# Causal masks added by the fused maximum on VectorE, and scores of 64-wide heads in pairs of row tiles

## The chip, the cores and the metric

The kernel runs on one core of one Trainium2 chip. The metric is device time in microseconds of one execution, from inputs in HBM to the output in HBM. TensorE, VectorE, ScalarE, GpSimd and SyncE each run their own stream of instructions; they meet only at semaphores.

## What is computed

Two layers of a "macaron" network over activations of 4 sequences x 512 tokens x 256 features. In order: attention with 64-wide heads and rotary positions (32 query heads, 8 key/value heads, causal over all 512 keys), a mixture of 16 experts, an attention with 8-wide heads and no mask; then the 64-wide attention and the experts once more, a gated block, an attention with 128-wide heads (16 query, 4 key/value heads, each block of 128 queries sees its own and the previous block of keys), and the gated block again. The part that matters here:

```
scores = einsum('bqhd,bkhd->bhqk', q, k) / sqrt(HEAD_DIM)
scores = where(causal, scores, -1e30)      # 128-wide: where(j >= p and j <= p + 128)
attn   = softmax(scores, -1)
o      = einsum('bhqk,bkhd->bqhd', attn, v)
```

Matrices are multiplied in split precision: each fp32 operand is kept as a rounded high part and a low part, and three products (high x high, low x high, high x low) replace one.

## The kernel before, in words

`Plan` writes one list of steps by hand. Every engine's program walks the whole list in that order and issues its share of each step, so the list fixes the order on each engine, and an engine that waits holds back everything behind it.

`Plan.attention` plans the attentions; `wide` is true for 128-wide heads. The 64-wide attention stands twice in the program ("narrow" here). It runs over 4 chunks `c` of heads x 4 sequences `b`: 16 units. A unit of the narrow attention has 8 groups, `(t, g)`: 4 query tiles `t` of 128 tokens, 2 key/value heads `g`. A group has 4 query heads `j`. It reads `o.w = (t + 1) * 128` keys. A unit of the wide attention has 4 groups of 4 heads with 128 or 256 keys. Inside a group, `Plan.attention` interleaves: the scores of this group's heads one at a time; `normalise` and `turn` (division by the sum, then the transposes of the probabilities, one step per 128 keys `kt`) of the group before; `weigh` (probabilities x values, column tiles of 64, every second group) and `project_out`; and four times `beside`, which issues pieces of the next unit's preparation (`q_product`, `q_rotate`, `k_rotate`, `v_copy` in one group; `q_turn`, `k_turn`, `k_low` and an empty piece in another). In the narrow attention TensorE has work in the first two of these four pieces only.

One head goes like this. TensorE writes scores into one PSUM bank (`scores`, L1442 on). Narrow: the transposed query tile holds the high part in partitions 0 to 63 and the low part in 64 to 127, one slot per head (copies L1712, L1713 on ScalarE, L1882, L1883 on VectorE); keys are stored twice, in both halves. So two products over 128 rows do the work of three: L1457 (times the high part of the keys) and L1458 (times the low part). A third product, L1461, adds the mask: a bfloat16 identity times 128 (wide: 256) columns of -1e30 and 0. VectorE takes the negated row maximum (L1895), ScalarE the exponential with its sum (L1723), which also frees the bank. `exponentials()` puts the exponentials of all waiting heads into the list at the place where it is called.

The banks for scores are a ring, `sring`: 3 for the narrow attention, 2 for the wide one. Head n of the narrow attention may start when the exponential of head n - 3 has ended. `tring` (2 banks) serves the transposes, which L1728 copies out; `wring` (3) serves the rest.

## Time and profile before

| | |
|---|---|
| median of 3 runs | 4043.11 us (4032.47 to 4050.41) |
| profiled execution, its time | 4029.73 us |
| span of the profiled execution | 4028.0 us |
| TensorE matmul busy | 3451.3 us, 86% |
| VectorE busy | 2704.4 us, 67% |
| ScalarE busy | 2025.5 us, 50% |
| granted TensorE clock, mean | 0.91 of full |
| narrow attentions | from about 50 to 1000 us and 1925 to 2870 us |
| wide attention | from about 3340 to 3910 us |

Busy time is the sum of the recorded durations of an engine's instructions. Matmuls overlap: a row's duration holds the time through the array, so the price of a matmul in a stream is the distance from its start to the next start. In the timelines, a bracket gives the idle time of the engine before the instruction and who ended it.

### The profile page before, as it was taken

To read this page: it belongs to the slowest core of one execution; us is meant where nothing else is said; L and a number is where in the kernel's file an instruction comes from. 1 tells how busy PE (TensorE), PEld (TensorE's weight loads), DVE (VectorE), ACT (ScalarE), POOL (GpSimd) and SP (SyncE) were. 2 spreads that over 40 slices of the span, in tenths; PEclk is the share of its full clock that TensorE was granted. 3 is DMA by queue.
4 is the path that set the end of the run, shared out by engine and by line. 5 is a ranking of instruction groups with operands and counts; after the bars stand their busy time and mean duration, and the time that the engine had idled before them with its cause. 6 is when DMAs were issued, how large, how long until landed. Compare 5 with 4: busy or idle time off the path is not lost. (4 is left out here: it accounts for less than half of the span.)

```text
span 4028.0 us, 61413 instructions
## 1 busy us (share of the span) xinstructions
PE 3451.3 (86%) x21258; PEld 2352.0 (58%) x21258; DVE 2704.4 (67%) x7549; ACT 2025.5 (50%) x5389; POOL 993.7 (25%) x964
## 2 busy tenths in 40 slices
PE   6899999887798599897789999988699668999986
PEld 4677677665454233343567767766455346788864
DVE  6788888775343677783778888876444456677766
ACT  4667767654222165665566767665322113455441
POOL 3211112232354100012121212123244332222213
PEclk9999999988899588998999999998799768999997
DMA  3140400011754322202050300001375500000010
GB/s 118 64 138 1 158 1 1 18 43 50 189 90 79 98 53 53 58 10 83 3 200 2 129 29 1 1 32 44 105 153 89 133 13 1 14 14 4 1 31 21
DMA packets 203899, 234.54 MB, mean 58 GB/s; under 512 B 20358, under 2 KB 190280, under 8 KB 202824
## 3 DMA queue, kind: packets, MB, share of 16 engines
q1 hardware_dynamic: 172648, 190.48, 15.5%
q0 software_dynamic: 30944, 40.14, 5.9%
q8 instruction: 172, 2.82, 0.3%
q14 instruction: 135, 1.11, 0.1%
HBM read 96.03 MB, written 133.73 MB: 57 GB/s over the span
## 5 line engine op out<-in xcount | busy, mean ns | idle before, releaser
L1723 ACT ACTIVATE p_prob<-bank,p_small 128x256 f32<-128x256 f32 (+3 forms) x1280 | 654.2, 517 | 240.0 <-DVE p_small L1895 223.6
L1895 DVE TENSOR_REDUCE p_small<-bank 128x1 f32<-128x256 f32 (+3 forms) x1280 | 586.8, 465 | 240.3 <-PE bank L1461 231.2
L1728 ACT ACTIVATE p_prT<-bank 128x512 f32<-128x512 f32 x752 | 420.3, 601 | 365.3 <-PE bank L1469 360.5
L2241 POOL TENSOR_TENSOR p_tm<-p_rope_a,p_rope_b 128x512 f32<-128x512 f32 x192 | 245.4, 1278 | 1437.6 <-DVE p_rope_b L1872 1420.7
L1469 PE MATMUL bank<-g_ident,p_prob 128*128 128x128 f32 x3008 | 440.8, 286 | 42.0 <-DVE p_prob L1904 21.4
L1457 PE MATMUL bank<-p_k,p_q 128*128 128x256 f32 (+2 forms) x1024 | 423.4, 414 | 53.8 <-ACT p_prob L1723 53.8
L1904 DVE TENSOR_SCALAR p_prob<-p_prob,p_small 128x256 f32<-128x256 f32 (+3 forms) x1280 | 417.1, 389 | 11.3
L1478 PE MATMUL bank<-p_prT,p_v 128*64 128x512 f32 (+1 forms) x1504 | 412.8, 604 | 0.2 <-ACT p_prT L1728 0.2
L1941 DVE TENSOR_REDUCE p_nmax<-bank 128x1 f32<-128x512 f32 x512 | 325.0, 684 | 101.1 <-PE bank L1519 95.6
L1469 PEld LDWEIGHTS bank<-g_ident,p_prob 128*128 128x128 f32 x3008 | 352.3, 147 | 63.6 <-DVE p_prob L1904 27.1
L1751 ACT ACTIVATE p_prT<-bank 128x512 f32<-128x512 f32 x512 | 278.0, 596 | 154.7 <-PE bank L1531 154.5
L1458 PE MATMUL bank<-p_k,p_q 128*128 128x256 f32 (+2 forms) x1024 | 339.8, 332 | 0.0
L1427 PE MATMUL bank<-p_w_hi,p_aT_hi 128*128 128x512 f32 (+1 forms) x768 | 298.8, 389 | 47.3 <-DVE p_aT_lo L1836 30.8
L1652 PE MATMUL bank<-p_w,p_hT 128*128 (+1 forms) x632 | 331.2, 607 | 0.2
L1461 PE MATMUL bank<-p_mask,g_identb 128*128 128x128 bf16 (+1 forms) x1280 | 310.1, 242 | 0.0
L1429 PE MATMUL bank<-p_w_lo,p_aT_hi 128*128 128x512 f32 (+1 forms) x768 | 267.0, 348 | 0.0
L1428 PE MATMUL bank<-p_w_hi,p_aT_lo 128*128 128x512 f32 (+1 forms) x768 | 267.0, 348 | 0.0
L1723 ACT ACTIVATION_READ_ACCUMULATOR p_prob<-bank,p_small 128x1 f32 x1280 | 265.8, 208 | 0.0
L1457 PEld LDWEIGHTS bank<-p_k,p_q 128*128 128x128 f32 x1024 | 203.4, 199 | 85.1 <-ACT p_prob L1723 71.1
L1490 PE MATMUL bank<-p_o_hi,p_oT_hi 128*128 128x256 f32 x768 | 233.9, 305 | 5.8 <-DVE p_oT_lo L1909 5.8
L1427 PEld LDWEIGHTS bank<-p_w_hi,p_aT_hi 128*128 128x128 f32 x768 | 151.9, 198 | 140.8 <-issue 76.3
L1869 DVE TENSOR_TENSOR p_rope_a<-bank,p_cos 128x512 f32<-128x512 f32 (+1 forms) x384 | 185.2, 482 | 69.1 <-PE bank L1429 69.0
(304 smaller groups left out, 7234.2 us busy)
## 6 DMA issues: line engine op xcount, KB each, us to landing
sorted<-p_blank SPq DMA_DIRECT2D x32, 2304.0 KB, 18.9
p_w<-in_L_ffn_w SPq DMA_DIRECT2D x96, 256.0 KB, 4.6
p_h_in<-sorted SPq DMA_DIRECT2D x158, 144.0 KB, 2.7
p_k_st<-k_saved SPq DMA_DIRECT2D x16, 288.0 KB
p_q_st<-q_saved SPq DMA_DIRECT2D x16, 288.0 KB
g_stage<-in_L_ffn_wq SPq DMA_DIRECT2D x8, 512.0 KB, 4.3
g_stage<-in_L_ffn_wo SPq DMA_DIRECT2D x16, 256.0 KB, 4.9
second_sum<-g_res SPq DMA_DIRECT2D x8, 512.0 KB, 5.6
```

Source lines behind the costliest of these rows:

```text
L1427: pe.matmul(use.ap[:, 0:n], hi, whi[:, k, cols(c0, n)], start=k == 0, stop=False)
L1457: pe.matmul(bank[:, 0:n], q[:, head, :], khi, start=True, stop=False)
L1458: pe.matmul(bank[:, 0:n], q[:, head, :], klo, start=False, stop=False)
L1461: pe.matmul(bank[:, o.w - mw:o.w], identb[:, :], A.mask[:, 2 * P - mw:2 * P], start=False, stop=True).then_inc(s.use.full[0].sem)
L1469: ins = pe.transpose(s.use.ap[:, j * P:(j + 1) * P], o.probs[j].ap[:, s.kt * P:(s.kt + 1) * P], ident[:, :])
L1478: ins = pe.matmul(s.use.ap[cols(o.g * A.hd, A.hd), :], o.u.v.ap[:, o.k0 + kt, cols(o.g * A.hd, A.hd)], o.prT[kt].ap, start=kt == 0, stop=k ...
L1652: ins = pe.matmul(o.up.ap, o.hT.ap[:, k * P:(k + 1) * P], w_all(A)[:, bass.ds(at + k * 2 * H, 2 * H)], start=k == 0, stop=k == KC - 1)
L1723: act.activation(s.prob.ap[:, 0:s.o.w], s.use.ap[:, 0:s.o.w], ACT.Exp, bias=sm[:, 0, j:j + 1], accum_out=sm[:, 1, j:j + 1]).then_inc(s.use ...
L1728: act.activation(s.prT.ap, s.use.ap, ACT.Copy).then_inc(s.use.free[0].sem)
L1895: dve.tensor_reduce(s.o.sm.ap[:, 0, s.j:s.j + 1], s.use.ap[:, 0:s.o.w], axis=AX.X, op=ALU.max, negate=True).then_inc(made)
L1904: dve.tensor_scalar(o.probs[j].ap[:, 0:o.w], o.probs[j].ap[:, 0:o.w], o.sm.ap[:, 2, j:j + 1], None, ALU.mult).then_inc(made)
L1941: dve.tensor_reduce(A.nmax[:, s.qt % 2, s.t, s.r, s.g % 2:s.g % 2 + 1], s.use.ap, axis=AX.X, op=ALU.max, negate=True).then_inc(s.use.free[ ...
```

## The change

Three edits, in all three attentions of these two kinds.

1. The mask product (L1461) and its bfloat16 identity go. VectorE's maximum becomes a `tensor_tensor_reduce`: it adds the mask (bfloat16, in SBUF; for narrow heads now 512 columns wide) to the scores, multiplies by -1, writes the result back over the scores in PSUM, and folds the minimum, which is the negated maximum. The exponential takes `scale=-1.0`.
2. Narrow: the query tile is laid out as the wide one: slots 0 to 3 high part, 4 to 7 low part, two heads per slot, one in partitions 0 to 63, the other in 64 to 127. One copy on ScalarE and one subtraction on VectorE over 128 partitions replace two each over 64.
3. Narrow: `scores` takes two heads at a time, (0, 1) and then (2, 3). TensorE waits for both banks, then issues three rounds, each with one product of 64 rows for either head: row tiles 0 to 63 and 64 to 127, different banks. The call for (0, 1) stands where head 0 stood and the call for (2, 3) where head 2 stood, ahead of `turn` for the key tiles 2 and 3; their exponentials come where those of head 2 came, behind these turns. Wide heads keep their order and their three products.

```diff
+        def scores(o, *heads):
             s = self.step("scores", A)
-            s.o, s.j, s.use, s.prob = o, j, sring.take(), prob.take()
+            for j in heads:
+                h.o, h.j, h.use, h.prob, h.max_made = o, j, sring.take(), prob.take(), self.vector_made.up()
+                waiting.append(h)
...
-                scores(cur, 0)
+                scores(cur, *((0,) if wide else (0, 1)))
...
-                scores(cur, 1)
+                if wide:
+                    scores(cur, 1)
...
                 exponentials()
-                scores(cur, 2)
+                scores(cur, *((2,) if wide else (2, 3)))
                 beside()
...
                 for kt in range(2, nturn):
                     turn(prev, kt)
                 exponentials()
-                scores(cur, 3)
-                exponentials()
+                if wide:
+                    scores(cur, 3)
+                    exponentials()
                 beside()
```

```diff
 # TensorE
-            w.wait_ge(s.use.before, *s.ready)
...
-                pe.matmul(bank[:, 0:n], q[:, head, :], khi, start=True, stop=False)
-                pe.matmul(bank[:, 0:n], q[:, head, :], klo, start=False, stop=False)
-            mw = min(o.w, 2 * P) if A.wide else P
-            w.wait_ge(A.masked)
-            pe.matmul(bank[:, o.w - mw:o.w], identb[:, :], A.mask[:, 2 * P - mw:2 * P],
-                      start=False, stop=True).then_inc(s.use.full[0].sem)
+            w.wait_ge(*(h.use.before for h in s.heads), *s.ready)
+            for i, (qp, kp) in enumerate(((0, 0), (4, 0), (0, 1))):
+                for h in s.heads:
+                    rows = slice(0, P) if A.wide else cols(h.j % 2 * A.hd, A.hd)
+                    at = qp + (h.j if A.wide else (o.g * KV + h.j) // 2)
+                    ins = pe.matmul(h.use.ap[:, 0:n], q[rows, at, :], k[rows, kp, o.g, keys], start=i == 0, stop=i == 2)
+                    if i == 2:
+                        ins.then_inc(h.use.full[0].sem)
 # VectorE
-            dve.tensor_reduce(s.o.sm.ap[:, 0, s.j:s.j + 1], s.use.ap[:, 0:s.o.w], axis=AX.X, op=ALU.max,
-                              negate=True).then_inc(made)
+            for h in s.heads:
+                x = h.use.ap[:, 0:o.w]
+                w.wait_ge(h.use.full, o.sm.after)
+                dve.tensor_tensor_reduce(x, x, A.mask[:, A.mask.shape[1] - o.w:], -1.0, FAR, ALU.add, ALU.min,
+                                         o.sm.ap[:, 0, h.j:h.j + 1]).then_inc(made)
```

## Rows read from the trace of the kernel before

**Rows 1.** Windows: length, busy us of PE, PEld, DVE, ACT, POOL, clock, DMA share, GB/s
```profile
300.00:400.00 100.00, 95.01 (x636) 71.54 (x635) 84.58 (x220) 72.62 (x199) 15.77 (x15) 1.00 0.00 1
...
3600.00:3700.00 100.00, 98.85 (x650) 81.26 (x650) 72.42 (x226) 50.04 (x162) 20.88 (x24) 1.00 0.00 1
```

**Rows 2.** Timeline, TensorE: first matmul of a narrow unit and of the next
```profile
341.61 0.37 PE L1457 MATMUL bank<-p_k,p_q 128*128 128x256 f32 x1
...
394.92 0.36 PE L1457 MATMUL bank<-p_k,p_q 128*128 128x256 f32 x1
```

**Rows 3.** Timeline, TensorE: a narrow head over 512 keys, and the next
```profile
439.07 0.48 PE L1457 MATMUL bank<-p_k,p_q 128*128 128x512 f32 x1
439.38 0.40 PE L1458 MATMUL bank<-p_k,p_q 128*128 128x512 f32 x1
439.62 0.23 PE L1461 MATMUL bank<-p_mask,g_identb 128*128 128x128 bf16 x1
439.74 0.50 PE L1457 MATMUL bank<-p_k,p_q 128*128 128x512 f32 x1
```

**Rows 4.** Timeline, all engines: 256-column heads, then a wait for a bank
```profile
355.48 0.36 PE L1457 MATMUL bank<-p_k,p_q 128*128 128x256 f32 x1
...
355.84 0.36 PE L1457 MATMUL bank<-p_k,p_q 128*128 128x256 f32 x1
...
356.26 0.36 ACT L1723 ACTIVATE p_prob<-bank,p_small 128x128 f32<-128x128 f32 x1
...
356.76 0.38 PE L1457 MATMUL bank<-p_k,p_q 128*128 128x256 f32 x1 [0.36 <-ACT p_prob L1723]
```

**Rows 5.** Timeline, TensorE: into the column tiles of `weigh` and out
```profile
348.81 0.23 PE L1461 MATMUL bank<-p_mask,g_identb 128*128 128x128 bf16 x1
348.97 3.65 PE L1478 MATMUL bank<-p_prT,p_v 128*64 128x512 f32 x16
352.56 0.50 PE L1427 MATMUL bank<-p_w_hi,p_aT_hi 128*128 128x512 f32 x1
```

**Rows 6.** Timeline, TensorE: row tiles in the attention with 8-wide heads
```profile
1501.47 0.50 PE L1531 MATMUL bank<-p_q_st,p_k_st 26*128 26x512 f32 x1
1501.47 0.50 PE L1519 MATMUL bank<-p_k_st,p_q_st 24*128 24x512 f32 x1
...
1501.91 0.39 PE L1541 MATMUL bank<-p_zero 128*128 128x256 bf16 x2
```

**Rows 7.** Timeline, weight loads: the load for L1458, beside the first row of Rows 3
```profile
439.15 0.19 PEld L1458 LDWEIGHTS bank<-p_k,p_q 128*128 128x128 f32 x1
```

**Rows 8.** Timeline, TensorE: a mask product of a wide head, and what follows
```profile
3592.49 0.28 PE L1461 MATMUL bank<-p_mask,g_identb 128*128 128x256 bf16 x1
3592.61 0.59 PE L1478 MATMUL bank<-p_prT,p_v 128*128 128x512 f32 x1
```

**Rows 9.** Groups: line, shapes, count, busy us, mean ns, idle before
```profile
L1895 DVE TENSOR_REDUCE p_small<-bank 128x1 f32<-128x256 f32 x448 | 184.7, 417 | 43.1 <-PE bank L1461 40.5
L1895 DVE TENSOR_REDUCE p_small<-bank 128x1 f32<-128x512 f32 x256 | 174.2, 687 | 92.8 <-PE bank L1461 91.1
L1723 ACT ACTIVATE p_prob<-bank,p_small 128x256 f32<-128x256 f32 x448 | 212.3, 476 | 161.9 <-DVE p_small L1895 155.5
L1723 ACT ACTIVATE p_prob<-bank,p_small 128x512 f32<-128x512 f32 x256 | 177.2, 700 | 10.6 <-DVE p_small L1895 5.0
L1883 DVE TENSOR_TENSOR p_q<-bank,p_q 64x512 fp32r<-64x512 f32 x128 | 88.9, 694 | 1.8
```

**Rows 10.** Timeline, VectorE: the fused operation in the experts
```profile
1097.67 0.17 DVE L2159 CUSTOM_DVE_ANT_0 p_pick<-p_h_in,p_one 128x16 f32<-128x16 f32 x1
1097.76 0.08 DVE L2159 DVE_READ_ACCUMULATOR2_ANT p_gate<- 128x1 f32 x1
```

**Rows 11.** Timeline, TensorE and ScalarE: two key tiles transposed, then copied
```profile
365.43 1.03 PE L1469 MATMUL bank<-g_ident,p_prob 128*128 128x128 f32 x8
...
366.07 1.09 ACT L1728 ACTIVATE p_prT<-bank 128x512 f32<-128x512 f32 x2 [1.90 <-PE bank L1469]
```

More of the change, by code:

```diff
@@ L167, in __init__ @@
         self.ident = top("ident", [P, P])
-        self.identb = top("identb", [P, P], BF16)
         self.half = top("minus_half", [P, NT])
@@ L204, in constants @@
         s = self.step("constants")
-        s.zeroed = [self.pool_made.up() for _ in range(2)]
-        s.made = [self.pool_made.up() for _ in range(3)]
+        s.zeroed = self.pool_made.up()
+        s.made = [self.pool_made.up() for _ in range(2)]
         self.constants_made = s.made[-1]
@@ L314, in attention @@
         A.lnw = sb("lnw", [P, KC])
-        A.mask = sb("mask", [P, 2 * P], BF16)
+        A.mask = sb("mask", [P, 2 * P if wide else S], BF16)
         if not wide:
@@ L323, in attention @@
         A.const = s.count.up(32 if wide else 48)
-        s.zeroed, s.right, A.masked = (self.pool_made.up() for _ in range(3))
+        s.zeroed, A.masked = self.pool_made.up(), self.pool_made.up()
+        if wide:
+            A.masked = self.pool_made.up()
         w_ready, o_ready, w_used, o_used = {}, {}, {}, {}
@@ L451, in group @@
             return o
-        def scores(o, j):
+        def scores(o, *heads):
             s = self.step("scores", A)
-            s.o, s.j, s.use, s.prob = o, j, sring.take(), prob.take()
-            s.ready = [o.u.q_made[o.t], o.u.k_made[max(1, o.t)]]
-            s.max_made = self.vector_made.up()
-            o.probs.append(s.prob)
-            o.scored = s.use.full
-            waiting.append(s)
+            s.o, s.heads, s.ready = o, [], [o.u.q_made[o.t], o.u.k_made[max(1, o.t)]]
+            for j in heads:
+                h = Phase()
+                h.o, h.j, h.use, h.prob, h.max_made = o, j, sring.take(), prob.take(), self.vector_made.up()
+                s.heads.append(h)
+                o.probs.append(h.prob)
+                o.scored = h.use.full
+                waiting.append(h)
         waiting = []
@@ L590, in attention @@
                 exponentials()
[L591 to L592 removed]
+                if wide:
+                    scores(cur, 3)
+                    exponentials()
                 beside()
@@ L1444, in tensor_program @@
         elif s.kind == "scores":
-            o, j, bank = s.o, s.j, s.use.ap
+            o = s.o
             n = max(o.w, 2 * P)
@@ L1893, in vector_program @@
         elif s.kind == "scores":
-            w.wait_ge(s.use.full, s.o.sm.after)
-            dve.tensor_reduce(s.o.sm.ap[:, 0, s.j:s.j + 1], s.use.ap[:, 0:s.o.w], axis=AX.X, op=ALU.max,
-                              negate=True).then_inc(made)
+            o = s.o
+            w.wait_ge(A.masked)
+            for h in s.heads:
[3 more added lines that the diff above has]
+                                         o.sm.ap[:, 0, h.j:h.j + 1]).then_inc(made)
         elif s.kind == "normalise":
@@ L2225, in pool_program @@
             w.wait_ge(own.turn())
-            pool.affine_select(out=A.mask[:, P:], in_=A.mask[:, P:], compare_op=ALU.is_ge, fill=NEG, base=0,
+            last = A.mask[:, A.mask.shape[1] - P:]
+            pool.affine_select(out=last, in_=last, compare_op=ALU.is_ge, fill=NEG, base=0,
                                pattern=[[-1, P]], channel_multiplier=1).then_inc(made)
-            w.wait_ge(own.turn())
-            pool.affine_select(out=A.mask[:, :P], in_=A.mask[:, :P], compare_op=ALU.is_ge, fill=NEG, base=0,
-                               pattern=[[1, P]], channel_multiplier=-1).then_inc(made)
+            if A.wide:
+                w.wait_ge(own.turn())
+                pool.affine_select(out=A.mask[:, :P], in_=A.mask[:, :P], compare_op=ALU.is_ge, fill=NEG, base=0,
+                                   pattern=[[1, P]], channel_multiplier=-1).then_inc(made)
         elif s.kind == "normed":
```

37 lines of the change are left out of this document (8 added, 29 removed).

## The prediction

> **What bounds the kernel now.** I read the table by slices first: the granted clock and the busy shares differ from stage to stage, so an edit is worth what it is worth in its own stage. Then the windows inside the stages that the change touches. In the steady part of the narrow attention TensorE is busy 95.0 of 100 us at full clock, VectorE 84.6, ScalarE 72.6; in the wide one TensorE is busy 98.9 [rows 1]. Both stages are bound by TensorE's order of work: what it does, plus what it waits for. Next the distance between the first matmuls of successive units: a narrow unit takes 394.92 - 341.61 = 53.3 us [rows 2], and there are 32 such units (2 attentions, 16 each). 5.0% of that, 2.7 us, is TensorE idle. Last the timeline around such a pause: a head that wants a bank waits until the exponential that holds it has ended [rows 4]. That wait is what the change rearranges.
>
> Prices on TensorE come from starts. A 512-column product takes 0.24 us of the stream, the mask behind it 0.12, a whole head 0.67 at its longest, as the first product behind a mask loses time to its weights (0.31 to the next start) [rows 3]; I take 0.64. A 256-column head takes 0.36 [rows 4], hence 0.12 for a product. For 384 columns I take the middle, 0.49 a head and 0.18 a product.
>
> **TensorE's work in a narrow unit.** Before: 16 heads x 0.36 (tiles 0 and 1 both stream 256 columns) + 8 x 0.49 + 8 x 0.64 = 14.8 us. After: 16 pairs of 3 rounds, 8 x 0.36 + 4 x 0.54 + 4 x 0.72 = 8.0 us, if the two row tiles run at once. Row tiles do so in the attention with 8-wide heads: two start in the same hundredth of a microsecond and take 0.50 each, as a lone one would [rows 6].
>
> But this visit to another tiling has a price. There a round of one 512-column product per tile holds the array from 1501.47 to 1501.91, 0.44 us, against 0.24 in a stream: 0.20 for weights that were not loaded ahead and for the array running empty at the end [rows 6]. Around `weigh` the same shows from outside: it starts 0.16 after the mask product, where the gap is otherwise 0.04 to 0.12, and the product behind it takes 0.50 instead of 0.40 [rows 3, 5]. So 0.2 us for each change of tiling. A unit has 16 visits, 32 changes. 4 fall away because the pair (0, 1) stands right before `weigh`, which changes tiling anyway. 8 fall away in the four groups where the group before had at most 2 key tiles: there nothing of TensorE stands between the pair (2, 3) and the next (0, 1). 20 x 0.2 = 4.0 us. TensorE's work shrinks by 14.8 - 8.0 - 4.0 = 2.8 us a unit. More than half of the gain in products and masks is eaten by changes of tiling.
>
> **The waits for banks.** With three banks and heads in pairs, the next group's pair (0, 1) needs the banks of this group's heads 1 and 2. Head 2 is scored last, together with head 3, and its exponential stands last too. Before, head 0 of the next group needed head 1 only, two heads back. So after the pair (2, 3) TensorE must wait for maximum and exponential of head 2, and what could cover it, the last two pieces of `beside`, holds no TensorE work in the narrow attention. Behind the wait are queued the pair itself, `weigh`, the products of the next unit and all transposes.
>
> The chain without cover: through the array 0.16 (0.40 of duration less 0.24 [rows 3]), 0.04 to VectorE, the maximum, 0.02 for the end of its accumulator read, 0.04 to ScalarE (three estimates, bounded by 0 and by the 0.14 that comes next), the exponential, and 0.14 until TensorE goes on (from 356.26 + 0.36 to 356.76 [rows 4]). The maximum of 256 keys takes 0.417, of 512 keys 0.687, the exponentials 0.476 and 0.700 [rows 9]; 128 keys: 0.28 by the same slope and 0.36 [rows 4]; 384: 0.55 and 0.59, the middles. Four groups have no cover: 128 keys 1.04, 256 keys twice 1.29, 384 keys 1.54; 5.2 us. In the other four, the turns of key tiles 2 and 3 stand between, but their copies stand ahead of the exponential on ScalarE. The first copy starts 0.64 after the first transpose, two copies take 1.09 and the next instruction starts about 0.1 before their end [rows 11]; 8 transposes cost TensorE 0.88 (1.03 less the 0.15 through the array), 4 cost 0.44. Two tiles: 0.64 + 0.97 + exponential 0.70 + 0.14 - 0.88 = 1.57, and with 128 keys 1.23. One tile: 0.64 + 0.5 + 0.14 - 0.44 + exponential = 1.43 (384 keys) and 1.54 (512). Sum 5.8.
>
> In addition the divisions of the group before stand behind two maxima instead of one on VectorE, 0.76 us later with 512 keys. In `q_turn` groups little TensorE work lies ahead of the transposes that need them: I add 0.9 us a unit for tiles 2 and 3, bounds 0 and 1.5. Waits after: 5.2 + 5.8 + 0.9 = 11.9 us against 2.7.
>
> **VectorE and ScalarE.** The fused operation is in the trace on 16 elements: 0.17 us, and the accumulator read starts 0.09 behind it and ends with it [rows 10]. So it adds little latency, but some 0.07 of VectorE a head: 32 x 0.07 = 2.2 us a unit. The low part of the queries saves one of two subtractions of 0.694 us, four times a unit, 4 x 0.63 = 2.5 us in a stream [rows 9]; ScalarE saves four copies of about 0.55, the size of those in [rows 11]. VectorE stays at 0.846 x 53.3 = 45 us a unit: even. No row shows the fused operation reading PSUM, taking a bfloat16 mask and writing PSUM. From below its rate is that of the plain maximum; no mechanism makes it faster. From above I take twice the time an element. I choose the lower end, since the only row of the operation has the fixed cost of a plain one.
>
> The smaller edits (bfloat16 identity, one select less, a mask of 512 columns) lie before the first scores, on GpSimd, and are costed at nothing, at most 1 us.
>
> **Wide.** 256 mask products go, 0.12 each [rows 8], 31 us, on an engine that is 98.9% busy [rows 1]. The order of heads stays. Shorter work on TensorE can make the waits on its two banks show: 15 to 31 us remain; I take 31.
>
> **Sum.** A regular narrow unit: 11.9 - 2.7 - 2.8 = +6.4 us. 24 units (chunks 0 to 2) give 154. In the 8 units of the last chunk the steps of the router hold TensorE between the same steps already, and a bank wait beside such a hold costs nothing; I take 4 of 6.4: 32. Narrow +186, wide -31: +155 us. On the profiled execution, 4029.7 us (span 4028.0), that is 4185; its time lies 13 under the median of the runs, so against the median 4043 + 155, rounded 4200. The sum is good to about a third of its waits: 11.9 could be 9 (-90 us over 32 units) or 14 (+67).
>
> **A rule of the skill on weights.** In the stream before, the weights for L1458 load at 439.15, while L1457 has run since 439.07 over the same 128 rows [rows 3, 7]: loads are hidden behind matmuls of the same rows, and I cost the rounds inside a visit so. The Trainium skill (TensorE: Matmul & The Clock Gate, "The mechanism" under packing small matmuls) says that a weight load overlaps running matmuls only when the row group differs. No row shows two rounds on the same row tile. If loads there were not hidden, as a mechanism of this kernel, each pair would pay its second and third load openly, 0.1 each (the 0.50 against 0.40 of [rows 3, 5]): 512 pairs x 0.2 = +102 us, 4300. That page's rule leads there; the trace contradicts it for full rows.
>
> **The rivals.**
> *Faster (0.10).* The waits in front of (0, 1) stay what they are, 2.7 us a unit, because maximum and exponential of head 2 are through by the time TensorE is: then 32 x 2.8 + 31 = 121 us are gained, 3920. For it: TensorE is the bound, and the masks are pure work on it. Against: the chain of two engines cannot be shorter than its two rows, and nothing covers it. It decides at waits of 2.7 + 2.8 + 1.0 (the wide gain per unit) = 6.5 us a unit, 0.8 per group; my smallest is 1.04.
> *No change (0.05).* The waits come to about that 6.5: 4025 to 4060.
> *The fused operation at half rate (0.07).* Write-back to PSUM adds 0.27 us for 256 keys, 0.53 for 512: about 1.8 us a unit in the open chains and, with 11 us more on VectorE, its own 56 us a unit come close to the period. About +4 us a unit, 4330.
> *Weights in the open (0.07).* 4300, as above.
> *Clock (0.07).* It is 1.00 in these windows [rows 1]; with pauses of 1.5 us in every group it could fall for parts of them. A tenth of 1700 us at half speed is +85 or so: 4285.
> *The pairs don't run together (0.02).* Then 8.0 us of rounds become 16: +256, 4455.
> *The forecast (0.62).* 4110 to 4290, likeliest 4200.
>
> **Numbers.** 0.5%, about what a measurement of this kernel can tell from no change, is 20 us. Slower: 0.62 + 0.07 x 3 + 0.02 = 0.85; same 0.05; faster 0.10. The range 4110 to 4320 holds forecast, clock and weights, and part of the half-rate case: about 0.8.
>
> **What would show it.** In the timeline of a narrow unit: a period near 60 us; TensorE idle before the first product of most groups until ScalarE's exponential, 1 to 1.6 us; that wait at the top of the list of waits, some 250 to 350 us in all. The two products of a round start together, rounds 0.12 or 0.24 apart, next work 0.1 to 0.2 late. The fused operation within 0.1 of the old maximum, a read of about 0.08. VectorE's busy time about even, ScalarE's lower by some 70 us (128 copies of 0.55). A wide unit shorter by up to 16 x 0.12 = 1.9 us. I am wrong if the pause after the pair (2, 3) is under 0.8 us, if rounds run slower than 0.24, or if the wide stage does not shrink.

## The result, and the profile after

| | before | after |
|---|---|---|
| median, same chip | 4046.76 us | 4240.01 us (4230.17 to 4249.77) |
| profiled execution | 4029.73 us | 4230.17 us |
| span | 4028.0 us | 4228.4 us |
| granted clock, mean | 0.913 | 0.909 |
| TensorE busy | 3451.3 us | 3395.0 us |
| VectorE busy | 2704.4 us | 2640.1 us |
| ScalarE busy | 2025.5 us | 1942.9 us |

The changed kernel takes 1.0482 of the time before (95% interval 1.0441 to 1.0523): 4.8% slower, where +155 us, 3.8%, was forecast. All three engines do less and the kernel takes longer, so the loss is waiting.

Measured from the first to the last score product of a stage in the two profiled executions: the two narrow attentions take 934.7 -> 1052.4 and 933.2 -> 1043.7 us (+228 together), the wide one 550.8 -> 530.9 (-20), everything else 1609.3 -> 1601.4 (-8). That is the 200 us between the spans.

The windows, in steady parts of a narrow and of the wide attention (columns as in [rows 1], which answers to them):

```profile
700.00:800.00 100.00, 82.12 (x566) 57.73 (x568) 71.16 (x249) 58.89 (x172) 14.06 (x14) 1.00 0.00 1
```
```profile
3800.00:3900.00 100.00, 98.19 (x633) 81.71 (x632) 75.39 (x279) 52.00 (x168) 20.98 (x24) 1.00 0.00 1
```

TensorE was busy 95.0 of 100 us in the narrow stage and is 82.1 now, at full clock. In the wide one it was 98.9 and is 98.2. What TensorE waits for stands on top of its list of waits (who waits, for whom, us in total, times, longest); before, this wait came to 53.8 us in 124 times:

```profile
PE bank L1460 <- ACT p_prob L1717: 318.7, 285, 2.8
PE bank L1625 <- DVE p_n_tiles L2061: 45.0, 18, 3.0
```

L1460 is the score product now, L1717 the exponential. A narrow unit, from its first matmul to that of the next, takes 807.01 - 747.45 = 59.6 us, against 53.3 in [rows 2]; a wide unit 3874.74 - 3842.01 = 32.7, against 34.05 before. Timeline, TensorE:

```profile
747.45 0.62 PE L1460 MATMUL bank<-p_k,p_q 64*128 64x256 f32 x6 [1.36 <-ACT p_prob L1717]
```
```profile
807.01 0.77 PE L1460 MATMUL bank<-p_k,p_q 64*128 64x256 f32 x6 [1.35 <-ACT p_prob L1717]
```
```profile
3842.01 0.99 PE L1460 MATMUL bank<-p_k,p_q 128*128 128x256 f32 x6
```
```profile
3874.74 0.76 PE L1460 MATMUL bank<-p_k,p_q 128*128 128x256 f32 x4
```

One open chain with 384 keys, all engines. The pair (2, 3) of a group is scored at 719.70, and the next group's pair (0, 1) follows at 721.91:

```profile
719.70 0.80 PE L1460 MATMUL bank<-p_k,p_q 64*128 64x384 f32 x6
720.53 0.57 DVE L1887 CUSTOM_DVE_ANT_0 bank<-bank,p_mask 128x384 f32<-128x384 f32 x1 [0.65 <-PE bank L1460]
721.01 0.14 DVE L1887 DVE_READ_ACCUMULATOR2_ANT p_small<- 128x1 f32 x1
721.01 0.60 DVE L1887 CUSTOM_DVE_ANT_0 bank<-bank,p_mask 128x384 f32<-128x384 f32 x1
721.19 0.58 ACT L1717 ACTIVATE p_prob<-bank,p_small 128x384 f32<-128x384 f32 x1 [0.73 <-DVE p_small L1887]
...
721.91 0.79 PE L1460 MATMUL bank<-p_k,p_q 64*128 64x384 f32 x6 [1.42 <-ACT p_prob L1717]
```

TensorE's row of six products ends at 720.50, VectorE begins 0.03 later, ScalarE follows 0.18 after the read's start, and TensorE goes on 0.14 after the exponential's end: 1.42 us in which TensorE has nothing that it may issue. The bank is head 2's; head 3's maximum runs beside it and holds nobody up.

The two engines whose work was exchanged, grouped by line and shape (columns as in [rows 9]):

```profile
L1887 DVE CUSTOM_DVE_ANT_0 bank<-bank,p_mask 128x256 f32<-128x256 f32 x448 | 185.6, 438 | 88.7 <-PE bank L1460 87.0
L1887 DVE DVE_READ_ACCUMULATOR2_ANT p_small<- 128x1 f32 x1280 | 181.7, 142 | 0.0
...
L1887 DVE CUSTOM_DVE_ANT_0 bank<-bank,p_mask 128x512 f32<-128x512 f32 x256 | 172.6, 716 | 169.5 <-PE bank L1460 169.5
```
```profile
L1896 DVE TENSOR_SCALAR p_prob<-p_prob,p_small 128x512 f32<-128x512 f32 x256 | 137.3, 600 | 2.3
```

The fused operation takes 438 and 716 ns where the plain maximum took 417 and 687 [rows 9], although it reads a mask and writes 128 x 512 scores back to PSUM. The division of 512 elements (L1896), which was not touched, went from 483 to 600 ns in the mean. Nothing in the forecast allowed for that; the trace leads to it below.

### The profile page after: what moved, and what is told of

The parts are those of the page before. It is cut to its first block and busy times, and to the rows that moved or that the text cites. A ratio compares the mean times of both kernels' runs of the same rounds, so it can differ in the third digit from the quotient of the medians.

```text
span 4228.4 us, 62424 instructions
## 1 busy us (share of the span) xinstructions
PE 3395.0 (80%) x21000; PEld 2237.8 (53%) x21002; DVE 2640.1 (62%) x8701; ACT 1942.9 (46%) x5261; POOL 992.5 (23%) x960
## 5 line engine op out<-in xcount | busy, mean ns | idle before, releaser
L1887 DVE CUSTOM_DVE_ANT_0 bank<-bank,p_mask 128x256 f32<-128x256 f32 (+3 forms) x1280 | 585.4, 491 | 509.9 <-PE bank L1460 482.6
L1460 PE MATMUL bank<-p_k,p_q 64*128 64x256 f32 (+3 forms) x3840 | 537.2, 354 | 325.6 <-ACT p_prob L1717 318.7
L1717 ACT ACTIVATE p_prob<-bank,p_small 128x256 f32<-128x256 f32 (+3 forms) x1280 | 644.7, 511 | 248.3 <-DVE p_small L1887 238.7
L1460 PEld LDWEIGHTS bank<-p_k,p_q 64*128 64x128 f32 (+1 forms) x3840 | 346.0, 193 | 449.1 <-ACT p_prob L1717 392.5
L1469 PE MATMUL bank<-g_ident,p_prob 128*128 128x128 f32 x3008 | 476.2, 292 | 48.5 <-DVE p_prob L1896 29.6
L1896 DVE TENSOR_SCALAR p_prob<-p_prob,p_small 128x256 f32<-128x256 f32 (+3 forms) x1280 | 426.5, 397 | 11.3
L1478 PE MATMUL bank<-p_prT,p_v 128*64 128x512 f32 (+1 forms) x1504 | 423.0, 620 | 0.2 <-ACT p_prT L1722 0.2
L1726 ACT ACTIVATE p_oT_hi<-bank 128x512 fp32r<-128x512 f32 x192 | 114.8, 598 | 391.6 <-PE bank L1478 370.8
L1717 ACT ACTIVATION_READ_ACCUMULATOR p_prob<-bank,p_small 128x1 f32 x1280 | 260.9, 204 | 0.0
L1491 PE MATMUL bank<-p_o_hi,p_oT_lo 128*128 128x256 f32 x768 | 225.5, 294 | 0.0
```

Of the source, the lines that this page charges most:

```text
L1460: ins = pe.matmul(h.use.ap[:, 0:n], q[rows, at, :], k[rows, kp, o.g, keys], start=i == 0, stop=i == 2)
L1469: ins = pe.transpose(s.use.ap[:, j * P:(j + 1) * P], o.probs[j].ap[:, s.kt * P:(s.kt + 1) * P], ident[:, :])
L1478: ins = pe.matmul(s.use.ap[cols(o.g * A.hd, A.hd), :], o.u.v.ap[:, o.k0 + kt, cols(o.g * A.hd, A.hd)], o.prT[kt].ap, start=kt == 0, stop=k ...
L1717: act.activation(s.prob.ap[:, 0:s.o.w], s.use.ap[:, 0:s.o.w], ACT.Exp, bias=sm[:, 0, j:j + 1], scale=-1.0, accum_out=sm[:, 1, j:j + 1]).th ...
L1887: dve.tensor_tensor_reduce(x, x, A.mask[:, A.mask.shape[1] - o.w:], -1.0, FAR, ALU.add, ALU.min, o.sm.ap[:, 0, h.j:h.j + 1]).then_inc(made)
L1896: dve.tensor_scalar(o.probs[j].ap[:, 0:o.w], o.probs[j].ap[:, 0:o.w], o.sm.ap[:, 2, j:j + 1], None, ALU.mult).then_inc(made)
```

## The experiments

Ratios are to the kernel before on the same chip, with the 95% interval. fused_only, fused_paired, after_4banks and covered ran on one chip in one batch; row_single, after_one_bank_less, after_exp_first and fused_exp_first on another; the last three ran on the first chip in a later batch. Where two runs of different batches are compared, both intervals count. "Unit" is the distance between the first matmuls of two successive narrow units in the steady part, 53.3 before and mostly 59.5, some 61.0, after. The theory: the loss comes from the order in pairs, in which head 2's bank is needed at once and nothing covers its chain. Against it stood the fused operation (rate, read, PSUM write), the row tiles (weights in the open, visits) and, once the traces were compared, VectorE's divisions.

**fused_only.** The fused maximum alone; heads one by one, products over 128 rows and the old query layout as before.

```diff
-                scores(cur, *((0,) if wide else (0, 1)))
+                scores(cur, 0)
...
+            for h in s.heads:
+                parts = ((h.j, 0), (4 + h.j, 0), (h.j, 1)) if A.wide else ((o.g * KV + h.j, 0), (o.g * KV + h.j, 1))
+                for i, (at, kp) in enumerate(parts):
+                    ins = pe.matmul(h.use.ap[:, 0:n], q[:, at, :], k[:, kp, o.g, keys], start=i == 0, stop=i == len(parts) - 1)
...
```

> The fused maximum alone: the order, the layout of the queries and the two products over 128 rows are those of the kernel before, heads one by one; only the mask products are gone and VectorE adds the masks. My theory (the order of the pairs costs the time, the fused maximum gains): TensorE loses 32 x 0.12 us of mask products a narrow unit and up to 1.9 us a wide unit, VectorE gains 2 us of work a unit; narrow unit 50 to 51.5 us instead of 53.3, wide unit 32.7 instead of 34.05, the whole 3920 to 3975 us. Rival (the fused operation, with its accumulator read, puts VectorE on the path in the narrow attention): narrow unit 53 to 56 us, the whole 4020 to 4110.

3951.97 us, ratio 0.9838 (0.9813 to 0.9862), unit 51.65. This is faster than both kernels. The gain of 1.65 us a unit is less than the masks' 32 x 0.12 = 3.8: TensorE is busy 2.7 us less in a steady unit (50.82 -> 48.11) and idle 1.0 us more (2.49 -> 3.52). A mask product in front of other work was worth less than 0.12: a lone head of 512 keys holds TensorE for 0.62 us before and 0.55 now, one of 256 keys 0.29 and 0.24 (medians of 94 and 154). And shorter heads wait longer for their banks (53.8 us in 124 times -> 86.1 in 140):

```profile
PE bank L1457 <- ACT p_prob L1719: 86.1, 140, 0.7
```

The rate of the fused operation and the mask from SBUF are cleared: the kernel that has them alone gains.

**fused_paired.** The same and the order in pairs, no row tiles and no new layout.

```diff
-                scores(cur, 0)
+                scores(cur, *((0,) if wide else (0, 1)))
...
-                scores(cur, 1)
+                if wide:
+                    scores(cur, 1)
...
-                scores(cur, 2)
+                scores(cur, *((2,) if wide else (2, 3)))
...
-                scores(cur, 3)
-                exponentials()
+                if wide:
+                    scores(cur, 3)
+                    exponentials()
```

> As the changed kernel, in its order of pairs, with the fused maximum, but the queries and the products over 128 rows of the kernel before: two products a head, no row tiles, no change of tiling. Theory (the bank wait behind the pair (2, 3) is the loss, not the row tiles): scores cost 10.6 us a narrow unit instead of 12.0, the waits stay; narrow unit 57.5 to 59.5 us, the whole 4170 to 4240. Rival (the row tiles and their changes of tiling are the loss): narrow unit near 51, the whole near 3960.

4237.26 us, ratio 1.0555 (1.0523 to 1.0587), unit mostly 62.0, some 60.4 and some 63.6, which is more than the 57.5 to 59.5 expected. Its wait is that of the changed kernel:

```profile
PE bank L1459 <- ACT p_prob L1721: 346.7, 289, 1.9
```

The order alone takes 0.9838 to 1.0555, 7.2 points or 285 us on one chip. Row tiles and the merged copies then bring back some 0.7 points: 1.0555 against 1.0482, two intervals that touch. The traces show where: a pair of 512 keys holds TensorE for 1.03 us in fused_paired and for 0.89 in the changed kernel, one of 384 keys 0.78 and 0.72, one of 256 keys 0.58 and 0.55.

**row_single.** The reverse: row tiles, new layout, but heads one by one.

```diff
-                scores(cur, *((0,) if wide else (0, 1)))
+                scores(cur, 0)
...
-                if wide:
-                    scores(cur, 1)
+                scores(cur, 1)
...
-                if wide:
-                    scores(cur, 3)
-                    exponentials()
+                scores(cur, 3)
+                exponentials()
```

> The changed kernel with heads one by one in the order of before: same layout of the queries, same 64-row products, three a head, but never two heads at once. Theory: no bank wait of the new kind, but 16 x 0.36 + 8 x 0.54 + 8 x 0.72 = 15.8 us of products and up to 32 visits to the row tiling at 0.4 us, 11 us net of neighbours, against 14.8 us of scores before: narrow unit 61 to 64 us, ratio 1.06 to 1.09. Rival (a visit to the row tiling costs TensorE next to nothing, and only the bank wait made the loss): narrow unit 51 to 53 us, ratio 0.98 to 1.00.

4166.34 us, ratio 1.0308 (1.0272 to 1.0344), unit 57.4: between the theory's range and the rival's. TensorE is busy 96 of 100 us and waits little, but with products that a single head cannot overlap:

```profile
300.00:400.00 100.00, 96.05 (x590) 65.48 (x590) 72.34 (x253) 61.21 (x176) 14.02 (x14) 1.00 0.00 1
```
```profile
701.38 0.96 PE L1458 MATMUL bank<-p_k,p_q 64*128 64x512 f32 x3
702.27 0.66 PE L1467 MATMUL bank<-g_ident,p_prob 128*128 128x128 f32 x4
702.86 0.97 PE L1458 MATMUL bank<-p_k,p_q 64*128 64x512 f32 x6
703.76 0.65 PE L1476 MATMUL bank<-p_prT,p_v 128*64 128x512 f32 x2
```

A lone head of 512 keys holds TensorE for 0.89 us, of which three products are 0.72; two heads issued one behind the other hold it for 0.90, so heads on different row tiles overlap even when they are issued in turn. A visit costs 0.17 beyond its rounds; its first product starts 0.20 after a transpose and 0.33 after a product of 512 columns, where it is 0.03 and 0.23 in fused_only. That is 0.27 to 0.35 a visit, less than the 0.4 (entry and exit) that the expectation of 61 to 64 used, and the expectation had no heads of two calls overlapping. Against fused_only (unit 51.6) the scores, with their third product, hold TensorE for 2.9 us a unit more, the work around them for 4.1 more, and it waits 1.3 less.

**after_4banks.** The changed kernel with four score banks in place of three, one fewer for the rest.

```diff
-        n_s = 2 if wide else 3
+        n_s = 2 if wide else 4
```

> The changed kernel with 4 banks for narrow scores instead of 3, and 2 instead of 3 for the other results. Theory: the pair (0, 1) needs only heads 0 and 1 of the group before, whose exponentials are long through; the 319 us of TensorE waiting for exponentials fall under 60, a narrow unit takes 49 to 54 us (the upper part is for what the missing third bank costs), the whole 3920 to 4070. Rival (the row tiles, or the fused operation's latency, make the time): within 1% of 4240.

4193.18 us, ratio 1.0437 (1.0418 to 1.0457), unit 58.9 to 60.4. The wait on exponentials fell from 318.7 to 7.4 us, as the theory says, but the unit fell far short of the 49 to 54 us expected. By the ratio the gain is 0.4 points, which lies within the 1% that the rival gave; so this run alone does not tell the two apart. Other waits stand in place of the one that fell:

```profile
PE bank L1447 <- DVE p_q L1872: 102.1, 88, 1.2
PE bank L1433 <- DVE p_rope_b L1866: 57.7, 35, 2.2
PE bank L1490 <- ACT p_v L1703: 47.1, 84, 0.7
PE bank L1433 <- DVE p_oT_lo L1901: 41.6, 56, 0.9
```

All four are waits for the banks of the remaining two. The run mixed two things, so the next one took them apart.

**after_one_bank_less.** Three score banks and two for the rest.

```diff
-        sring, tring, wring = (Banks(self.banks[i:j]) for i, j in ((0, n_s), (n_s, n_s + 2), (n_s + 2, 8)))
+        sring, tring, wring = (Banks(self.banks[i:j]) for i, j in ((0, n_s), (n_s, n_s + 2), (n_s + 2, 8 if wide else 7)))
```

> Control for the run with 4 score banks: the changed kernel with 3 score banks and 2 banks for the other narrow results; the eighth bank is left unused in the narrow attentions. With 4 + 2 banks the waits of scores for exponentials vanished, but waits of 286 us for the two remaining banks stood in their place. Theory (both waits are real, and the score wait is worth its price where nothing else binds): this one has both kinds; narrow unit 63 to 66 us, the whole 4330 to 4450 at the level of this chip's before of about 4020. Rival (the score wait is no loss of its own, TensorE would be held by VectorE's and ScalarE's work anyway): narrow unit within 1 us of the 58.9 of the run with 4 + 2 banks, the whole within 1% of 4193.

4499.94 us, ratio 1.1156 (1.1134 to 1.1178), unit 67 to 69.5, more than the 63 to 66 expected. At two other banks the fourth score bank is worth 1.1156 - 1.0437 = 7.2 points; at three score banks the third other bank is worth 1.1156 - 1.0482 = 6.7. A score bank more is worth about the whole cost of the order, and so is a bank for the rest: the kernel has no bank to give. That a ninth bank would take the loss away is argued from these differences, not shown; and whether a fourth score bank would also help heads issued one by one was not run.

**after_exp_first.** Head 2's and 3's exponentials ahead of the turns of key tiles 2 and 3.

```diff
+                if not wide:
+                    exponentials()
                 for kt in range(2, nturn):
                     turn(prev, kt)
                 exponentials()
```

> The changed kernel with one call moved: in narrow groups the exponentials of heads 2 and 3 stand ahead of the turns of key tiles 2 and 3 instead of behind them, so ScalarE does them ahead of the copies. Theory by the sum of the forecast: the four groups without such turns stay as they are; in the other four the copies leave the chain, 0.97 us in two groups, 0.5 us in two, less what the copies themselves then come late: narrow unit 57 to 58.5 instead of 59.5, ratio to before 1.030 to 1.042. If the order on ScalarE doesn't matter: 1.048.

4095.53 us, ratio 1.0154 (1.0123 to 1.0185), unit 56.4: more than the 1.030 to 1.042 that the expectation gave. TensorE's wait fell by 99 us:

```profile
PE bank L1462 <- ACT p_prob L1719: 219.8, 224, 1.5
```

3.3 of the 4.8 points hang on where ScalarE's copies of the turned probabilities stand. In the steady unit the four open waits are what they were (0.94, 1.18, 1.18, 1.42 us), and the four behind turns fell from 5.05 us to 1.91. That is 24 x 3.1 = 74 us from 59.5 to 56.4, of some 133. The last chunks of the two attentions give 39 us. The rest is in what changed beside it: no unit of 61 us is left, and the time at half clock in the narrow stages is 91 and 81 us in place of 137 and 126.

**covered.** The pair (2, 3) ahead of the second piece of `beside` and of all turns, its exponentials ahead of the copies.

```diff
+                if not wide:
+                    scores(cur, 2, 3)
                 beside()
+                if not wide:
+                    exponentials()
                 for kt in range(0, min(2, nturn)):
                     turn(prev, kt)
                 exponentials()
-                scores(cur, *((2,) if wide else (2, 3)))
+                if wide:
+                    scores(cur, 2)
```

> The changed kernel with another order in narrow groups: the pair (2, 3) right behind project_out, ahead of the second piece of preparation and of all turns, its exponentials ahead of the copies of the turns. So that piece (0.2 or 0.7 us) and all turns (0.4 to 1.8 us) stand between the pair (2, 3) and the next pair (0, 1). Theory: the wait for the exponential of head 2 is covered in most groups; a narrow unit takes 49.5 to 52.5 us, the whole 3910 to 4010. If the wait isn't the cause: within 1% of 4240.

4071.93 us, ratio 1.0138 (1.0109 to 1.0167), unit 57.0 to 59.0; 49.5 to 52.5 was expected. The cover works, and TensorE meets the next resource, the two banks of the transposes:

```profile
PE bank L1474 <- ACT p_prT L1727: 129.5, 119, 2.2
PE bank L1465 <- ACT p_prob L1722: 88.1, 113, 2.9
```

The copies that free the transposes' banks now stand behind two exponentials.

**covered_full.** The same order, products over 128 rows and the old query layout.

```diff
-            for i, (qp, kp) in enumerate(((0, 0), (4, 0), (0, 1))):
-                for h in s.heads:
-                    rows = slice(0, P) if A.wide else cols(h.j % 2 * A.hd, A.hd)
+            for h in s.heads:
+                parts = ((h.j, 0), (4 + h.j, 0), (h.j, 1)) if A.wide else ((o.g * KV + h.j, 0), (o.g * KV + h.j, 1))
...
```

> The order with the pair of heads 2 and 3 put ahead of the second projection piece and the turns (as in the run covered, ratio 1.0138), with products over 128 rows and no row tiles. The theory that the order sets the loss and that the row tiles and merged copies are worth 1 to 2.4 us of a narrow unit once the order is pairwise: unit 58 to 59.5 against 57.0, ratio 1.020 to 1.032. Rival: with its exponentials covered this order is bound by the tiling changes' visits, so without row tiles it gains: unit 55 to 56.5, ratio 0.998 to 1.012.

4116.38 us, ratio 1.0201 (1.0161 to 1.0240), unit 57.2 to 58.5 with some to 62. So row tiles and merged copies are worth some 0.6 points in this order too, as in the first pair of runs (0.7); the two intervals touch in both pairs, so the size is rough. The ratio lies at the low end of what the theory gave, and outside the rival's; the steady unit is shorter than the 58 to 59.5 of the theory. In the profiled executions the gain stands here in the last chunk (33 of 38 us), while in the first pair it stands in the other units (21 us) and the last chunk loses 29. Last chunks differ by some 12 us an attention between executions where their steps are the same (fused_split_moved below), so this split decides little.

**fused_exp_first.** The fused maximum alone, with the exponential of head 1 ahead of the first turns.

```diff
+                if not wide:
+                    exponentials()
                 for kt in range(0, min(2, nturn)):
                     turn(prev, kt)
                 exponentials()
```

> The fused maximum alone, heads one by one over 128 rows, with the exponential of head 1 ahead of the turns of key tiles 0 and 1 instead of behind them. The fused-only kernel waits 86 us on TensorE for exponentials, in 140 places, where head 0 of the next group needs the bank of head 1. Theory: that wait goes at the groups with one key tile, 30 to 80 us less: ratio to before 0.965 to 0.977 against 0.984. If TensorE is held by something else there (the copies of the turns, now late): 0.98 to 0.99.

3992.82 us, ratio 0.9896 (0.9879 to 0.9912), unit 52.3: worse than without (0.9838, 0.9813 to 0.9862), and not the 0.965 to 0.977 that the theory gave. The wait on exponentials halved (86.1 -> 40.1) and a new one took its place:

```profile
PE bank L1467 <- ACT p_prT L1726: 72.4, 87, 2.8
PE bank L1459 <- ACT p_prob L1721: 40.1, 90, 1.7
```

**after_split_moved and fused_split_moved.** For the units of 66 to 71 us that the forecast did not have: GpSimd's splits of the next block's weights (L2202) behind the first group of the unit with b = 2, in the changed kernel and in fused_only.

```diff
-            if b == 2 and c + 1 < NU:
-                split_qkv(c + 1, slot_qkv)
-                split_o(c + 1, slot_o)
...
                 prev = cur
+                if (t, g) == steps[0] and b == 2 and c + 1 < NU:
+                    split_qkv(c + 1, slot_qkv)
+                    split_o(c + 1, slot_o)
```

What led there is VectorE's timeline in such a unit of the changed kernel, and GpSimd's beside it, and TensorE's:

```profile
433.79 7.00 DVE L1896 TENSOR_SCALAR p_prob<-p_prob,p_small 128x512 f32<-128x512 f32 x4
```
```profile
434.54 3.48 POOL L2202 TENSOR_TENSOR p_w_lo<-g_stage,p_w_hi 128x1536 fp32r<-128x1536 f32 x1 [18.66 <-ACT p_w_hi L1690]
438.17 2.34 POOL L2202 TENSOR_TENSOR p_o_lo<-g_stage,p_o_hi 128x1024 fp32r<-128x1024 f32 x1
```
```profile
438.36 0.33 PE L1469 MATMUL bank<-g_ident,p_prob 128*128 128x128 f32 x1 [1.34 <-DVE p_prob L1896]
440.85 0.77 PE L1469 MATMUL bank<-g_ident,p_prob 128*128 128x128 f32 x5 [2.15 <-DVE p_prob L1896]
```

Four divisions of 512 elements take 7.00 us, while elsewhere in this kernel four take 1.67. The held ones end 0.3 us behind the two splits, and TensorE's transposes wait for them.

> The changed kernel with GpSimd's splits of the next attention block's weights placed behind the first group of the unit with b = 2 instead of ahead of that unit; nothing else differs. Theory: in the changed kernel the divisions of a group meet these splits on VectorE's and GpSimd's common memory path (four divisions in 7.00 us where others take 0.5 each), and this is what makes the units with b = 2 of the narrow attentions 66 to 71 us against 59.5 to 61. Moved, the splits meet matmul-bound or waiting stretches, the units fall to 60 to 62, and with six or so of them 30 to 45 us go: ratio to the kernel before 1.037 to 1.041. Rival: the splits only collide with other VectorE work in the later groups (copies out of banks, subtractions), so the loss moves along: ratio 1.045 to 1.052, and the unit stays at 66 to 71.

4206.89 us, ratio 1.0425 (1.0397 to 1.0452), against 1.0482 (1.0441 to 1.0523) unmoved. The two units at 432 and 680 us that took 66.1 and 67.3 take 61.0 and 59.5, the one of 71.1 takes 64.9. The spans differ by 27 us: the narrow attentions take 43 us less (2096.1 -> 2053.0), the wide one 2 less, and what lies outside the three attentions, where the edit changes nothing, 18 more. So the units bear the mechanism out. The ratio is just above the 1.037 to 1.041 expected, and its interval overlaps the unmoved one's. The collision itself did not go, it moved to divisions of 128 elements, and TensorE's waits for divisions fell from 29.6 to 20.0 us:

```profile
434.04 4.14 DVE L1896 TENSOR_SCALAR p_prob<-p_prob,p_small 128x128 f32<-128x128 f32 x4
```
```profile
434.62 3.47 POOL L2202 TENSOR_TENSOR p_w_lo<-g_stage,p_w_hi 128x1536 fp32r<-128x1536 f32 x1 [2.09 <-ACT p_w_hi L1690]
```

Four such divisions take 0.88 us when no split runs.

> The kernel with the fused maximum alone (heads one by one, products over 128 rows) and the same move of GpSimd's splits. Theory of the collision: long divisions (over 1 us) cost the kernel before some 13 us beyond their usual 0.48 us each, so at most about 10 us are to be had: ratio 0.981 to 0.984. Rival: heads one by one keep banks waiting for TensorE and not the other way round, the collision is covered, and the move gives nothing (0.984) or brings the splits into a stretch that was tight (up to 0.990).

3987.93 us, ratio 0.9878 (0.9858 to 0.9898): the rival. The units with b = 2 in the middle of fused_only already took 51.65, so nothing was there to be had, and after the move they take 52.6. The rest of what it lost, some 3 us a unit in the mean of the last chunks (267.5 -> 278.0 and 266.8 -> 280.9), where the step list is the same, I can't attribute. The kernel with heads one by one and the fused maximum alone, 0.9838, remains the best that was run.

## Why the forecast was right, and where its terms were off

**The waits (11.9 us a unit forecast).** The mechanism is what the traces show, and after_exp_first, fused_paired and the two bank runs each confirm a part of it. The unit was forecast at 59.7 and takes 59.5. The eight waits in front of a pair (0, 1) are 1.09, 0.94, 1.18, 1.18, 1.42, 1.25, 1.36 and 1.36 us in the unit at 747.45, 9.8 in all, against 10.9 in the forecast's sum; that sum counts 0.16 through the array in each, which the profile counts as busy, so on one count they agree within 0.2. The 0.9 us for late divisions is not what the trace shows: the other two waits of the unit come to 0.79 us, and a wait for the copies of turned probabilities (0.47 of it) was there before with 0.74. Windows of one steady unit, before and after:

```profile
341.61:394.92 53.31, 50.82 (x339) 37.59 (x338) 43.77 (x116) 37.07 (x106) 8.03 (x8) 1.00 0.00 1
```
```profile
747.45:807.01 59.56, 49.00 (x337) 34.07 (x337) 41.30 (x152) 34.47 (x101) 8.03 (x8) 1.00 0.00 1
```

TensorE's idle time rose by 8.1 us, where 9.2 were forecast, and its busy time fell by 1.8, where 2.8 were forecast. With the 8 x 0.16 = 1.3 us through the array counted as busy, the forecast says 7.9 and 1.5: two of its terms hold, not only their sum. That the unit comes out within 0.2 us is still partly luck, since the 0.9 for divisions stood for other waits.

**TensorE's work (-2.8 a unit forecast).** Right in kind. The pairs run together (the first two products of a pair start 0.003 us apart); of the rounds of 512 columns the second starts 0.33 behind the first, the third 0.23 behind the second. A pair over 512 keys, with the transposes of the next step behind it:

```profile
734.93 0.96 PE L1460 MATMUL bank<-p_k,p_q 64*128 64x512 f32 x6
735.82 0.44 PE L1469 MATMUL bank<-g_ident,p_prob 128*128 128x128 f32 x2
```

735.82 - 734.93 = 0.89, of which 0.72 are rounds. The other 0.17 lie half between the first two rounds and half behind the third. The entry costs 0.1 to 0.2 more (0.10 after a product of 512 columns, 0.18 after a transpose, by row_single against fused_only). So a visit costs 0.27 to 0.35, less than the 0.4 forecast, while masks in front of other work were worth less than the 0.12 taken (fused_only): two misses of opposite sign. The two experiments in pairs without row tiles put row tiles and merged copies at 0.6 to 0.7 points, 25 to 30 us. The forecast held visits to eat more than half of what row tiles save. In row_single visits, the third product, which a lone head can't overlap, and more time at half clock (331 us in the narrow stages against 193 in fused_only) together cost 4.7 points (1.0308 against 0.9838).

**The rule on weights.** The loads of a pair, and those for `weigh` behind it:

```profile
721.91 0.47 PEld L1460 LDWEIGHTS bank<-p_k,p_q 64*128 64x128 f32 x6 [1.74 <-ACT p_prob L1717]
722.63 0.20 PEld L1478 LDWEIGHTS bank<-p_prT,p_v 128*64 128x64 f32 x4 [0.25 <-issue]
```

The products of this pair start in rounds at 721.91, 722.19 and 722.37 and end at 722.70. All six loads are through at 722.38. The first round's products are in the array until 722.35, so those for the second and third round began while products over the same two row tiles were still in it. One distance is 0.10 longer than a round of 384 columns (0.28 against 0.17), not two, and that is in the 0.17 to 0.19 of a visit already. So the Trainium skill's rule (TensorE: Matmul & The Clock Gate, "The mechanism") that a load overlaps running matmuls only on another row group is not what this trace shows, for row tiles as for full rows, and the rival at 4300 us falls.

**VectorE.** The fused operation within 0.03 of the old maximum: right. The accumulator read was put at 0.08, from 16 elements [rows 10], and takes 0.142, always. It overlaps the next fused operation (both start at 721.01). In a steady unit of fused_only VectorE is busy 44.89 us against 43.77 before, so the fused operations cost 1.1 us a unit instead of the 2.2 forecast. In the changed kernel's unit it is 41.30, and VectorE's busy time, forecast about even, fell by 64 us in all. ScalarE fell by 83, forecast 70.

**The last chunk (4 us a unit forecast, 6.5 measured).** The 24 units of chunks 0 to 2 lost 176 us (154 forecast), the 8 of the last chunk 52 (32 forecast). In the second unit of that chunk the last six groups take 57.7 us before and 56.9 after. That seems to bear out the step "a bank wait beside such a hold costs nothing". But the granted clock there is 0.82 before and 0.92 after, 10.4 and 4.6 us of work lost, so the waits may have cost what the clock gave, and the step is not shown. The first two groups take 16.4 and then 22.3. Windows over these two groups, of before and of after:

```profile
778.30:783.30 5.00, 5.00 (x28) 4.39 (x28) 4.09 (x19) 1.78 (x6) 2.35 (x2) 0.73 0.09 30
783.30:794.70 11.40, 11.03 (x74) 7.62 (x72) 6.98 (x25) 5.26 (x18) 8.36 (x10) 1.00 0.26 92
```
```profile
877.00:899.30 22.30, 18.53 (x96) 12.57 (x96) 9.62 (x40) 7.01 (x24) 10.06 (x10) 0.80 0.15 53
```

By the granted clock, 0.20 of 22.3 us is 4.5 us of work lost to half clock, against 0.27 of 5.0 = 1.4 before: 3.1 of the 5.9. The others are pauses, 3.8 us idle against 0.4. So the forecast's 4 us left the clock out in a stretch where TensorE had just been held.

**What the forecast did not have.** The 176 us are 24 x 6.2 = 149 and 27 more. Part is the collision of divisions and splits: with the splits moved, chunks 0 to 2 take 33 us less. It was there before: the sum of what divisions of probabilities over 1 us take beyond their usual time was 9 us, in the changed kernel it is 30, in after_exp_first 14. Before, the last large division starts with the split (398.28 and 398.30) and only small ones meet it; the order in pairs puts the last two of four large divisions under the splits. The other part is clock. In some units TensorE runs at half clock behind the first pair, in others it doesn't. Windows, and one matmul in each, of two units of the changed kernel:

```profile
748.00:750.00 2.00, 2.00 (x13) 1.73 (x12) 1.86 (x9) 0.88 (x5) 0.00 (x0) 1.00 0.00 0
...
808.00:810.00 2.00, 2.00 (x5) 1.52 (x5) 1.96 (x9) 0.81 (x4) 0.00 (x0) 0.50 0.01 4
```
```profile
748.34 0.39 PE L1434 MATMUL bank<-p_w_hi,p_aT_lo 128*128 128x512 f32 x1
748.58 0.39 PE L1435 MATMUL bank<-p_w_lo,p_aT_hi 128*128 128x512 f32 x1
```
```profile
808.30 0.63 PE L1434 MATMUL bank<-p_w_hi,p_aT_lo 128*128 128x512 f32 x1
808.73 0.63 PE L1435 MATMUL bank<-p_w_lo,p_aT_hi 128*128 128x512 f32 x1
```

The same two products are 0.24 apart at 748 and 0.43 at 808, and the granted clock is 1.00 and 0.50, the levels of 2.4 and 1.2 GHz. Such a stretch lasts some 3 us and makes a unit of 59.5 into one of 61.0. Ahead of both TensorE idles 1.36 and 1.35 us. Time at half clock rose in the narrow stages from 101 and 85 us to 137 and 126. Collisions and clock are not independent: with the splits moved the time at half clock is 88 and 101 us, about that of before. So I don't split the 27 us further.

**Wide (-31 forecast, -20 measured).** The unit fell from 34.05 to 32.7, 1.3 of the 1.9 that 16 masks of 0.12 would give. The forecast took the whole and named the reason for less, waits on the two banks; the waits of a wide score product for its exponential are 7.3 us in the changed kernel:

```profile
L1460 PE MATMUL bank<-p_k,p_q 128*128 128x256 f32 x768 | 136.1, 299 | 8.4 <-ACT p_prob L1717 7.3
```

It was 5.1 us before, so this wait explains 2 of the missing 11. Over the stage (3344.93 to 3895.69 before, 3564.28 to 4095.16 after) TensorE's busy time fell from 533.7 to 508.3 us, 25 instead of 31, and its idle time rose from 17.0 to 22.6. The step that was too large is the price of a mask: a lone wide head holds TensorE for 0.50 us before and 0.44 after, two in succession for 0.96 and 0.72 (medians of 125 and 64), so 0.12 a mask only where heads follow each other, and 0.06 in front of other work. The measured 20 lies within the 15 to 31 given.

**The sum.** +155 forecast, +200 measured in the profiled executions: narrow +228 (+186), wide -20 (-31), elsewhere -8 (0). The missing 42 us in the narrow attentions are 20 in the last chunk and 22 in the other units.

## What to carry to other kernels

In a ring of n banks, n - 1 heads lie between a head and the one whose bank it takes when they are issued one by one, and n - 2 when they are issued in pairs; whoever frees that bank then stands on the path. Before pairing, lay the chain of the last member end to end (here 0.9 to 1.4 us of idle TensorE) and ask which work of the bound engine stands beside it: if none does, the pairing costs that chain in each group, and a faster product gives back a fraction. Try the parts alone: here one of three edits gained 1.6%, and all three together lost 4.8%.

## What the runs showed of the hardware

- VectorE's divisions (tensor_scalar, fp32, SBUF to SBUF) stand still while an elementwise operation of GpSimd runs: 3.7 us for one that otherwise takes 0.48, four of them 7.00 where 1.67 is usual. A short rotary addition of GpSimd holds them too. In the kernel before, the first of four divisions of 128 elements (1.46 us) ends 0.09 behind a split, the third (1.32 us) 0.08 behind an addition of 1.27 us, and the four take 3.10 us where 0.88 is usual:

```profile
403.25 3.10 DVE L1904 TENSOR_SCALAR p_prob<-p_prob,p_small 128x128 f32<-128x128 f32 x4
```
```profile
402.26 2.36 POOL L2213 TENSOR_TENSOR p_o_lo<-g_stage,p_o_hi 128x1024 fp32r<-128x1024 f32 x1
404.80 1.27 POOL L2241 TENSOR_TENSOR p_tm<-p_rope_a,p_rope_b 128x512 f32<-128x512 f32 x1 [0.17 <-POOL p_o_lo L2213]
```

  The one that comes second waits: a division that runs when a split starts (398.28 and 398.30) takes its usual 0.48, and that split takes 3.82 us, against 3.42 for the one at 10.14, when VectorE does nothing. The Trainium skill (SBUF — State Buffer, "SBUF: two separate sides") has VectorE and GpSimd share one pair of ports that the first holds for a whole operation; these rows agree with that.
- The fused add, scale and minimum reads PSUM and a bfloat16 mask and writes PSUM at nearly the rate of the plain maximum (438 against 417 ns for 256 columns, 716 against 687 for 512). Its accumulator read takes 142 ns, and the next operation starts beside it.
- Two products of 64 rows on different row tiles start within 0.003 us and hold TensorE as one; a visit to them costs 0.17 to 0.19 beyond its rounds and 0.1 to 0.2 ahead of them. Heads issued one behind the other on different row tiles overlap too: 0.90 us for two of 512 keys where one takes 0.89, though 0.96 against 0.72 with 384 keys.
